# A graph network's two weighted edge sweeps: scatter products placed between the weights products, and constant products on TensorE ahead of its waits

## What is computed

```python
# first layer (the last one has a second hidden layer of 64 and silu in place of relu)
h = jax.nn.relu(edge_feat @ W1 + b1)                 # (E, 32) -> (E, 64)
w = (h @ W2 + b2).reshape(e, 4, MUL, MUL)            # 256 weights for each edge
s_e, v_e = s[src], v[src]                            # row of the source node
m0 = ALPHA * (einsum('ei,eio->eo', s_e * sh0, w_000) + C110 * einsum('eim,em,eio->eo', v_e, sh1, w_110))
m1 = ALPHA * (einsum('ei,em,eio->eom', s_e, sh1, w_011) + einsum('eim,eio->eom', v_e * sh0, w_101))
out0 = jax.ops.segment_sum(m0, dst, num_segments=n)
out1 = jax.ops.segment_sum(m1.reshape(e, MUL * 3), dst, num_segments=n)
x = _layernorm(x + ...)
```

## Time and profile before

| what | us |
|---|---|
| the three runs | 18744.48, 18747.74, 18798.73 |
| their median | 18747.74 |
| the profiled execution: its own time, as far as given (fastest run) | 18744.48 |
| its span, first to last instruction | 18741.8 |
| first weighted sweep, its 628 blocks | 5352 (from 90 to 5442) |
| coupled sweep | 5166 (from 5550 to 10716) |
| second weighted sweep, its 628 blocks | 5447 (from 13229 to 18676) |

### The profile page before, as it was taken

The page is one execution under the profiler, slowest core; times in us unless marked ns, Lnnn a source line. Parts: engine busy times, 40 slices in busy tenths (PEclk is TensorE's granted clock), DMA queues, the critical chain, the costliest instruction groups (busy, mean ns, idle before and its releaser), DMA issues. The chain is left out here.

```text
span 18741.8 us, 308593 instructions
## 1 busy us (share of the span) xinstructions
PE 14220.5 (76%) x89407; PEld 10314.7 (55%) x89407; DVE 12292.2 (66%) x24385; ACT 5069.6 (27%) x12977; POOL 9141.7 (49%) x9516
## 2 busy tenths in 40 slices
PE   6877777777766666666666689899778888888887
PEld 4554555555546666656565667676444444444444
DVE  6666766666665565655565558578666666666666
ACT  1111111111123333333333357476211111111112
POOL 4555555555545555555555400100455555555554
PEclk7777777777765555555555569789788887888887
DMA  1111111111111111111111056365011111111111
GB/s 33 21 21 20 22 21 20 21 20 21 21 20 15 15 15 15 15 15 15 15 15 15 14 173 212 121 222 178 15 13 13 13 13 13 13 13 14 14 13 14
DMA packets 1106496, 699.39 MB, mean 37 GB/s; under 512 B 853332, under 2 KB 1021953, under 8 KB 1105890
## 3 DMA queue, kind: packets, MB, share of 16 engines
q1 hardware_dynamic: 802236, 541.65, 10.2%
q0 software_dynamic: 304160, 156.34, 6.5%
HBM read 680.89 MB, written 16.07 MB: 37 GB/s over the span
## 5 line engine op out<-in xcount | busy, mean ns | idle before, releaser
L598 PE MATMUL weighted_weights_ps<-weighted_w_out,weighted_hidden 128*128 128x256 f32 x12600 | 4494.0, 490 | 6.3 <-DVE weighted_to_s L723 3.2
L428 POOL DMA_INDIRECT weighted_rows<-x_after_convolved,weighted_idx x3140 | 3054.3, 973 | 2483.1 <-DMA weighted_sh<-in_sh 1568.6
L428 POOL DMA_INDIRECT weighted_rows<-in_x,weighted_idx x3140 | 3026.6, 964 | 2398.9 <-DMA weighted_sh<-in_sh 1471.6
L859 POOL DMA_INDIRECT coupled_rows<-x_after_weighted,coupled_idx x3125 | 2956.2, 946 | 2206.2 <-DMA coupled_sh<-in_sh 1230.5
L598 PEld LDWEIGHTS weighted_weights_ps<-weighted_w_out,weighted_hidden 128*128 128x128 f32 x12600 | 2641.7, 232 | 2262.4 <-issue 1957.5
L870 PE MATMUL coupled_win<-coupled_onehot,coupled_prod 128*125 128x64 f32 x12500 | 2602.4, 398 | 892.1 <-issue 554.9
L870 PEld LDWEIGHTS coupled_win<-coupled_onehot,coupled_prod 128*125 128x125 f32 x12500 | 2528.1, 312 | 943.4 <-issue 584.1
L588 PE MATMUL weighted_hid_ps<-weighted_feat,weighted_w_in 32*64 32x320 f32 (+1 forms) x3786 | 1754.3, 549 | 1256.1 <-ACT weighted_hidden L647 791.0
L631 PEld LDWEIGHTS weighted_win_ps<-weighted_onehot,weighted_prod 128*128 128x128 f32 x12560 | 1945.5, 226 | 121.8
L718 DVE TENSOR_TENSOR weighted_v_v<-weighted_weights_ps,weighted_scaled 128x320 f32<-128x320 f32 x3768 | 1957.3, 574 | 0.0
L647 ACT ACTIVATE weighted_hidden<-weighted_hid_ps,weighted_b_in 64x320 f32<-64x320 f32 x1262 | 659.6, 523 | 4728.0 <-remote 2067.5
(11 more groups left out here) (225 smaller groups left out, 16040.4 us busy)
## 6 DMA issues: line engine op xcount, KB each, us to landing
cells_src<-cell_sources SPq DMA_DIRECT2D x496, 800.0 KB
weighted_feat<-in_ef SPq DMA_DIRECT2D x635, 80.0 KB
weighted_rows<-in_x,weighted_idx POOLq DMA_INDIRECT x3140
weighted_rows<-x_after_convolved,weighted_idx POOLq DMA_INDIRECT x3140
coupled_rows<-x_after_weighted,coupled_idx POOLq DMA_INDIRECT x3125
weighted_idx<-in_src_blocks SPq DMA_DIRECT2D x1264, 2.5 KB
weighted_sh<-in_sh SPq DMA_DIRECT2D x1264, 10.0 KB
coupled_sh<-in_sh SPq DMA_DIRECT2D x630, 22.5 KB
```

What stands on the lines that cost most here:

```text
L428: pool.indirect_dma_start(rows[s][:, t, :], None, table, bass.IndirectOffsetOnAxis(ap=idx[s][:, t:t + 1].bitcast(U32), axis=0))\
L598: mm = pe.matmul(banks[bank][:, t * WPATHS:(t + 1) * WPATHS], hidden[slot][:, t * P:(t + 1) * P], w_out[:, :], start=True, stop=True)
L859: pool.indirect_dma_start(rows[s][:, t, :], None, table, bass.IndirectOffsetOnAxis(ap=idx[s][:, t:t + 1].bitcast(U32), axis=0))\
```

## The change

The scatter of block n moves out of its place behind `both` into `both`: each of its five products stands ahead of one weights product of block n + 3. Its sum goes into 64 unused columns (`WIN_AT`, 1280) of the very bank group that these weights go to, so `w_ready` of block n + 3 covers both, and `win_ps`, `spread` and the wait for it are gone. VectorE adds the window three blocks late (`BEHIND = 3`), right behind line 732 and ahead of the last read of the weights, from the bank it is reading anyway. TensorE now runs one block further ahead: hidden products of block n + 4, weights products of n + 3. The turns stay 157 and the blocks 628, since three blocks without edges were there already; the additions for the last blocks at the end of the pass are gone. The bank that `win_ps` had is now `steady_ps`: between the first hidden product and the wait for the weights bank (`keep_clock`), TensorE multiplies a constant bf16 tile of ones (128 x 512) with itself, five times a block in the shallow sweep, twice in the deep one. Nothing reads the result.

The core of the diff:

```diff
-BEHIND = 1
+BEHIND = 3
+STEADY = 512
+STEADY_SHALLOW, STEADY_DEEP = 5, 2
@@ weighted_edges
-        win_ps = psum("win", [P, 512])
+        steady, steady_ps = sb("steady", [P, STEADY], BF16), psum("steady", [P, STEADY])
@@ tensor
+                def weight_gate(b):
+                    pe.wait_ge(hidden_ready, (b + 1) * PER_BLOCK)
+                    if not isinstance(b, int) or b >= 2:
+                        pe.wait_ge(w_used, b + 1)
+                def spread_mm(slot, bank, t):
+                    pe.matmul(banks[bank][0:MSG, WIN_AT:WIN_AT + WINDOW], prod[slot][:, t, :], onehot[slot][:, t, :],
+                              start=(t == 0), stop=(t == TILES - 1))
+                def keep_clock():
+                    for _ in range(STEADY_DEEP if deep else STEADY_SHALLOW):
+                        pe.matmul(steady_ps[:, :], steady[:, 0:P], steady[:, :], start=True, stop=True)
@@ both
                     hidden_mm(b_h, slot_h, 0)
-                    weight_mm(b_w, slot_w, bank_w, [0, 1])
-                    hidden_mm(b_h, slot_h, 1)
-                    weight_mm(b_w, slot_w, bank_w, [2, 3])
-                    if deep:
-                        hidden_mm(b_h, slot_h, 2)
-                    weight_mm(b_w, slot_w, bank_w, [4])
+                    keep_clock()
+                    weight_gate(b_w)
+                    if spread is not None:
+                        pe.wait_ge(msg_ready, b_w - BEHIND + 1)
+                    for t in range(TILES):
+                        if spread is not None:
+                            spread_mm(spread, bank_w, t)
+                        weight_mm(slot_w, bank_w, t)
+                        if t == 1:
+                            hidden_mm(b_h, slot_h, 1)
+                        if deep and t == 3:
+                            hidden_mm(b_h, slot_h, 2)
@@ loop
-                            both(n + 3, (s + 3) % SLOTS, g + (s + 3) // SLOTS, n + 2, (s + 2) % SLOTS, s % 2)
-                            pe.wait_ge(summed, n + p * BEHIND + 2)
-                            pe.wait_ge(msg_ready, n + 1)
-                            for t in range(TILES):
-                                mm = pe.matmul(win_ps[0:MSG, 0:WINDOW], ...)
-                            mm.then_inc(spread, 1)
+                            both(n + 4, s, g + 1, n + BEHIND, (s + BEHIND) % SLOTS, (s + BEHIND) % 2, s)
@@ vector
                             last.then_inc(vec, 1)
+                            if s == 0:
+                                bases = win.bases(i * SLOTS)
+                            add_window(n, banks[s % 2], bases[s])
                             dve.wait_ge(vec, n * VEC + 3)
...
-                            add_window(n + 1, n + p * BEHIND, bases[s])
                             dve.wait_ge(vec, n * VEC + 5)
```

57 lines of the change are left out of this document (24 added, 33 removed).

## The result

The changed kernel takes 19,044 us (median of 4 runs, 18,988 to 19,085), the kernel before 18,746 (4 runs, 18,705 to 18,799): a ratio of 1.0165, 95% interval 1.0134 to 1.0196. Slower by 1.65%, where 7% faster was forecast; the range held the time, the direction was wrong.

What follows compares the result with a forecast made beforehand. No engine was full; late signals left TensorE dry and at half clock. Blocks of 6.25 + 1.2 and 6.34 + 1.2 us saved 673 and 712 us, setup cost 8: 17,370 us, range 16,300 to 19,100.

Steps and rivals of the forecast that it cites:

- Scatter and addition: Weighted sweeps: VectorE's addition no longer waits for its round's scatter; 4 us of cover for late weights signals.
- What remains: Late signals left in each weighted block: 1.2 us taken, from 0.1 to the coupled sweep's 1.63.
- The floor: Slowest engine per weighted block: 6.25 us (gathers) in the first sweep, 6.34 (TensorE) in the second.
- the sign: Weighted sweeps: a mean clock over 0.9 would show the prediction right.
- TensorE's round at full clock: With the constant products added: 6.04 us in the first weighted sweep, 6.34 in the second.
- the interleaved scatter at zero: Scatter between weights products on TensorE: 0 to +0.3 us a round thought possible, 0 taken.
- the round at half clock: TensorE, first weighted sweep: 11.5 us with the constant products in place of 9.4.
- The slower one: Weighted sweeps: clock still falls behind late signals, constant products paid at half clock; 19,530 us, chance 0.21.
- the forecast 630 for the first sweep: Constant products paid at half clock in the first weighted sweep: 296 rounds at +2.13 us.
- the path takes it all back: Weighted sweeps: signal path limited to 5.8 to 6.2 instructions per us, added ones eat the gain; 18,750 us, chance 0.10.
- The signal path as a fixed rate: Weighted sweeps: TensorE limited to 7.36 instructions per us; 17,680 us, chance 0.19.
- It all works: Weighted sweeps: remaining waits under 0.2 us a block; 15,990 us (below 16,300), chance 0.05.

Runs made afterwards that it cites:

- h2: Changed kernel without constant products, scatter together behind the weights products, still added three blocks late; chip with late signals: 18,921 us, 0.9957 of before.
- g0: Kernel before, with ScalarE delayed (one extra 5.00 us activation in every fourth block of both weighted sweeps): 15,713 us.
- g1: Changed kernel, with ScalarE delayed (one extra 5.00 us activation in every fourth block of both weighted sweeps): 16,400 us.
- h3: Changed kernel without constant products, scatter behind the weights products, second hidden bank, ScalarE delayed every fourth block; chip with late signals: 19,332 us.
- f3: Changed kernel with the weighted sweeps' gathers replaced by one plain DMA a block; signals on time: 14,355 us, 0.9826 of before.
- e3: Changed kernel with its constant columns in four times as many products (20 and 8 of 128 columns); signals on time: 14,711 us, 1.0102 of before.
- f0: Kernel before, unchanged, profiled again on a chip with signals on time: 14,613 us, ratio 1.0010.
- f1: Changed kernel, unchanged, on a chip with signals on time: 14,638 us, 1.0031 of before.
- i1: Changed kernel without constant products, scatter together behind the weights products; chip with signals on time: 14,697 us, 1.0101 of before.
- g2: Changed kernel without constant products, ScalarE delayed (one extra 5.00 us activation in every fourth block): 16,538 us.

## Why the prediction failed

**The step that failed** is in *Scatter and addition*: "That leaves 4 us of cover for a late signal, where the addition had none to spare." Both halves are wrong. Four microseconds are there only if TensorE stands at its gate, the wait for `w_used` ahead of the weights products, that is, if it is ahead of VectorE. It never was: its waits there are 6.3 us of the first sweep before the change and 0.0 after. The 6.3 us stood in the trace of the kernel before and could have been asked for. The prediction had a further reason of its own, a round of 6.04 us with the constant products against VectorE's block of 5.83. But that is not the whole of it, since h2, with a round without constant products, has no lead either. And the order before did have something to spare: g0 covers 3.0 of 5.0 us in the first sweep, g1 0.2.

The runs show in its place that TensorE was the path, and VectorE's wait for the scatter a consequence of it. TensorE's time is its busy time and its wait for ScalarE. The late signal goes to ScalarE as well, which I named but never priced: 4.31 us of TensorE's standstill in the timeline, 894.6 in the first sweep of the changed kernel and 1180.8 before. Moving the scatter and the addition leaves that wait where it was (1169.3 in h2's first sweep), and a second hidden bank (h3) is what shortens it. What the change added to TensorE's work, 521 us in the first sweep, is more than the 293 us of waiting that it took away. How much of the 521 is the five constant products, which take 1073.3 us there, and how much the interleaving, no run on a chip with late signals separates.

**What remains** was a term of 1.2 us a block. It measured (886.2 + 268.9) / 628 = 1.84 and (1029.6 + 272.2) / 628 = 2.07, above the upper bound of 1.63 and above before's 1.69 and 1.39.

**The floor** took TensorE's own lateness as zero, since the clock would be full. It measured 745.9 / 628 = 1.19 and 469.4 / 628 = 0.75 us, at a mean clock of 0.82 and 0.87 where over 0.9 was to be the sign. First sweep: 5.82 busy + 1.84 + 1.19 = 8.85 us of the 8.89 a block in place of 7.45; second 5.82 + 2.07 + 0.75 = 8.64 of 8.67, in place of 7.54. Before, the same three were 5.83 + 1.69 + 0.90 and 5.85 + 1.39 + 1.33.

**Right by size:** TensorE's round at full clock (6.01 and 6.30 in f3; 6.04 and 6.34 forecast), the interleaved scatter at zero, and the round at half clock, 11.42 us (forecast 11.5), of which the five constant products are 2.11 (2379.78 to 2381.89; forecast 2.13):

```profile
2378.55 1.29 PE L592 MATMUL weighted_hid_ps<-weighted_feat,weighted_w_in 32*64 32x320 f32 x2 [3.81 <-ACT weighted_hidden L660]
2379.78 2.31 PE L615 MATMUL weighted_steady_ps<-weighted_steady 128*128 128x512 bf16 x5
2381.89 0.52 PE L608 MATMUL weighted_weights_ps<-weighted_onehot,weighted_prod 128*128 128x64 f32 x2
...
2389.97 1.32 PE L592 MATMUL weighted_hid_ps<-weighted_feat,weighted_w_in 32*64 32x320 f32 x2
```

**The rivals.** The slower one had the direction and its mechanism in part: holes stay (ScalarE's remote time is 1963.5 us in the first sweep, 2067.5 before), and constant products are paid at half clock. With 0.36 of 5580 us at half clock and 11.42 us a round that is 176 rounds at 2.13, 375 us, an estimate, against the forecast 630 for the first sweep; less of the time was at half clock than it feared. "Slower by 1.65%" lies between it (19,530) and "the path takes it all back" (18,750). The signal path as a fixed rate did not show: 6.5 instructions per us here, in either sweep, 13.6 in e3. "It all works" has a slip in its sum: 7943 + 628 x 6.5 x 2 is 16,107, not 15,990. The 38041 instructions of the coupled sweep are 38043. Neither touches the forecast.

ScalarE's group in the first sweep, of the kernel before (not shown ahead) and of the changed one:

```profile
L647 ACT ACTIVATE weighted_hidden<-weighted_hid_ps,weighted_b_in 64x320 f32<-64x320 f32 x1256 | 656.5, 523 | 4698.0 <-remote 2067.5 <-PE weighted_hid_ps L588 1849.5 <-issue 781.0
```

```profile
L660 ACT ACTIVATE weighted_hidden<-weighted_hid_ps,weighted_b_in 64x320 f32<-64x320 f32 x1258 | 656.8, 522 | 4925.1 <-PE weighted_hid_ps L592 2379.8 <-remote 1963.5 <-issue 581.8
```

**Not settled:** what makes signals late. The traces leave a mark: that of before holds 125,267 records of semaphore changes, f0's 293,660 for the same program; h2's, on the other late chip, 120,838. More than half of these records are missing where signals are late, while those of instructions are all there (308,593 in either trace). The Trainium skill ("NOTIFIC — the notification-queue block", 7.1 Overflow) says that a full queue of records drops new ones or stalls their producer, by how it is set. Missing records fit the first and late signals the second, so one queue with one setting does not explain both by that page. It is a coincidence of two marks, no proof. A run on a late chip without gathers was not had, and whether the recording itself has a part in the lateness was not asked.

## What to carry to other kernels

Before costing a late signal as covered, ask who is ahead of whom, and read it from the trace: an engine that has a lead waits at the gate that its consumer opens. Here TensorE's wait at that gate was 6.3 us in a sweep of 5352, so there was no lead to spend, and the place to look was where it did wait (1180.8 us, ahead of the products that need ScalarE). A long wait on the consumer's side (VectorE's 1630 us) does not say that the consumer's order is at fault. Profile the kernel on a second chip before tuning against a wait named "remote": this one is 22% faster where signals are on time, and there the change costs 0.3%. And a lateness put in by hand, on a fixed beat, prices an order's tolerance in one run.

## What the hardware showed beyond that

A gather isn't always 0.94 us. One that starts beside VectorE's one-hot is longer. Timeline of f1, first sweep, GpSimd and VectorE:

```profile
2004.35 0.94 POOL L430 DMA_INDIRECT weighted_rows<-in_x,weighted_idx  x1 [0.30 <-issue]
2005.49 0.48 DVE L470 TENSOR_TENSOR weighted_onehot<-weighted_iota,local 128x320 f32<-128x320 f32 x1
2005.59 1.20 POOL L430 DMA_INDIRECT weighted_rows<-in_x,weighted_idx  x1 [0.30 <-issue]
2006.71 0.28 DVE L715 TENSOR_TENSOR weighted_vsh<-weighted_rows,weighted_sh 128x120 f32<-128x120 f32 x1 [0.74 <-DMA weighted_rows<-in_x,weighted_idx]
...
2012.07 0.48 DVE L470 TENSOR_TENSOR weighted_onehot<-weighted_iota,local 128x320 f32<-128x320 f32 x1
2012.11 1.27 POOL L430 DMA_INDIRECT weighted_rows<-in_x,weighted_idx  x1 [0.30 <-issue]
```

The pattern feeds itself: VectorE waits 0.74 us for the long gather's rows, and so its next one-hot falls on a gather again, 6.58 us later. Of the 3120 gathers of f1's first sweep, the 137 that start beside the one-hot (L470) take 1180 ns in the mean, and the 288 that start beside the message's last product (L750), which the one-hot follows, 1261. Those that start beside a product with the weights (L725, L732, L740) take 943 or 944. In f1's first sweep a gather takes 991 ns in the mean, in f0's 962; 3121 x (991 - 962) ns = 91 us are about the loss of f1 against f0 there (4073 to 3987). i1's take 995 and 996 in its two sweeps against f0's 962 and 957, and its second sweep is 4085 us long against f0's 3963, where 3120 x 39 ns make 122 (i1's profile is of its slowest run, 14,806 us). The Trainium skill ("GPSIMD Engine Reference", 1. Specifications) says that GpSimd's interfaces to SBUF (where the kernel's `sb` tiles lie) are contended by VectorE instructions with two SBUF inputs. The trace agrees: L470 and L750 have two, while the products with the weights read one of theirs from a bank of `weights`, not from SBUF.

Half clock can last while TensorE has no gap: 32.8 us of it in g2 with TensorE busy for 32.77. g0's two sweeps have 157 stretches at half clock each, as many as there are latenesses. With the scatter products between the weights products and no constant products it stayed down for 17.9 us in the mean of g2's first sweep, with the scatter behind them for 6.9 in g0's. In the second sweep, which has a third hidden product in the round, it was 6.8 in both, so the place of the scatter does not settle it alone.
